# A recursive edge-list GNN kernel: a fourth pair list with its own stage, a third table of deep sums, and six matrix-power passes over 24 gather tiles in place of seven over 40

## The reference, cut to what matters

```
def step(f, _):
    msg = f[src] * edge_weight[:, None]
    agg = segment_sum(msg, dst, num_segments=n)
    return (1.0 - ALPHA) * agg + ALPHA * feat_0, None      # K = 10 steps, ALPHA = 0.1
x = layernorm(x + scan(step, x, K))
```

## Time and profile before

| what | value |
|---|---|
| median of 3 runs | 4958.19 us (4956.72 to 4958.65) |
| the profiled execution's own time | 4952.22 us |
| its span, first to last instruction | 4950.1 us |
| busy: PE, DVE, POOL, ACT | 2892, 3047, 2596, 1262 us |
| share of q1 (SP and ACT queues' DMAs), q0 (POOL's) of 16 DMA engines | 30.2%, 14.2% |

### The profile page before, as it was taken

The page is one execution under the profiler, slowest core; times in us unless marked ns, Lnnn a source line. Parts: engine busy times, 40 slices in busy tenths (PEclk is TensorE's granted clock), DMA queues, the critical chain, the costliest instruction groups (busy, mean ns, idle before and its releaser), DMA issues. The chain is left out here.

```text
span 4950.1 us, 60862 instructions
## 1 busy us (share of the span) xinstructions
PE 2892.4 (58%) x9882; PEld 1516.2 (31%) x9882; DVE 3047.2 (62%) x7896; ACT 1261.6 (25%) x3891; POOL 2596.0 (52%) x2528
## 2 busy tenths in 40 slices
PE   4700000577776999999999566656222210897665
PEld 3500000233332666666666211111111100333332
DVE  8989990788886777777777444433233326564333
ACT  0133330232332444444444111111100002342111
POOL 0067777555552233333333477747465560565776
PEclk9955555777777999999999688778555555997555
DMA  2067762899998454444444255533333324232111
GB/s 65 0 176 216 217 206 50 139 148 149 147 146 145 130 136 131 130 135 128 134 133 128 68 142 145 140 68 64 56 48 48 46 36 113 65 73 49 38 38 27
DMA packets 735672, 526.54 MB, mean 106 GB/s; under 512 B 526161, under 2 KB 647962, under 8 KB 730594
## 3 DMA queue, kind: packets, MB, share of 16 engines
q1 hardware_dynamic: 582822, 381.10, 30.2%
q0 software_dynamic: 92160, 102.50, 14.2%
q10 hardware_dynamic: 60612, 42.15, 4.0%
HBM read 270.21 MB, written 261.82 MB: 107 GB/s over the span
## 5 line engine op out<-in xcount | busy, mean ns | idle before, releaser
L1224 POOL DMA_INDIRECT out<-xob,ob x400 | 426.6, 1067 | 813.0 <-DVE xob L1327 716.5
L486 POOL DMA_INDIRECT xdst<-in_x,dstc x400 | 457.4, 1143 | 402.1 <-PEq L634 260.7
L270 POOL DMA_INDIRECT gb<-nodes,ib x400 | 393.2, 983 | 289.2 <-ACT ib L841 190.0
L259 PE MATMUL bank<-ident,act 128*99 128x128 f32 x400 | 87.1, 356 | 767.9 <-DVE act L985 698.5
L283 PE MATMUL bank<-l_chosen,l_rec 128*3 128x512 f32 x480 | 310.1, 807 | 119.3 <-DVE l_chosen L277 119.3
L290 PE MATMUL bank<-chosen,rec 128*6 128x512 bf16 x1200 | 377.9, 481 | 1.5 <-DVE chosen L277 1.5
L270 POOL DMA_INDIRECT cgb<-layer,ib x160 | 176.1, 1100 | 252.4 <-ACT ib L2102 205.2
L259 PEld LDWEIGHTS bank<-ident,act 128*99 128x99 f32 x400 | 66.4, 224 | 775.6 <-issue 775.6
L1249 PE MATMUL bank<-hm,w 128*112 128x512 f32 x600 | 301.1, 640 | 0.0
L264 PE MATMUL bank<-ident,scan 99*128 99x99 f32 (+2 forms) x1120 | 198.8, 307 | 145.6 <-DVE scan L1915 101.9
L1266 PE MATMUL bank<-bxT,w 121*128 121x512 f32 x600 | 276.5, 597 | 11.9 <-ACT bxT L1176 11.9
(11 more groups left out here) (296 smaller groups left out, 7468.3 us busy)
## 6 DMA issues: line engine op xcount, KB each, us to landing
nodes<-wt SPq DMA_DIRECT2D x40, 1286.2 KB
edges<-gb ACTq DMA_DIRECT2D x100, 194.0 KB
run_rows<-tb SPq DMA_DIRECT2D x100, 194.0 KB, 6.3
xa<-run_rows SPq DMA_DIRECT2D x100, 194.0 KB, 3.3
kb<-edge_keep SPq DMA_DIRECT2D x100, 192.0 KB
lsb<-edges SPq DMA_DIRECT2D x200, 96.0 KB
deep_sum<-bzeros SPq DMA_DIRECT2D x50, 384.0 KB
layer<-bzeros SPq DMA_DIRECT2D x50, 384.0 KB
```

What stands on the lines that cost most here:

```text
L259: last = nc.tensor.transpose(slot(dst_ps[0:w, :], t), rows_sb[:, t, c0:c0 + w], ident[:, :])
L270: yield nc.gpsimd.indirect_dma_start(out=dst[s][:, t, 0:width], out_offset=None, in_=table, in_offset=bass.IndirectOffsetOnAxis(ap=ib[s][: ...
L486: nc.gpsimd.indirect_dma_start(out=xdst[:, k * F:(k + 1) * F], out_offset=None, in_=a["x"], in_offset=bass.IndirectOffsetOnAxis(ap=dstc[:, ...
L1224: nc.gpsimd.indirect_dma_start(out=out, out_offset=bass.IndirectOffsetOnAxis(ap=ob[s][:, t:t + 1], axis=0), in_=xo[s][:, t, :], in_offset= ...
```

## The change

It adds a level. `level(2)` now takes the form that `level(1)` had (it builds list 3 and scatters its sums to `deep_sum[1]`) with two slots, `prepare(3)` follows, and `level(3)` takes the form without a list. `steps` works on list 3 and goes through six passes. The end pass scatters to a new table, `deep_sum[2]`, which is cleared beside the others and added in the merge. Tables and arrays are renamed and rotated accordingly. The core of the diff:

```
-LU = (4, 4, 2)
+LU = (4, 4, 2, 2)
-LZ = 15 * LW // P
+LZ = 19 * LW // P
...
+                      edges.rearrange("(e w) -> e w", w=PW), nodes[0:half].rearrange("(e w) -> e w", w=F)]
+        swap_rows = edges[0:half].rearrange("(e w) -> e w", w=F)
...
-        deep_sum = [dram(f"deep_sum{k}", (EP + 1, F)) for k in range(2)]
+        deep_sum = [dram(f"deep_sum{k}", (EP + 1, F)) for k in range(3)]
...
-                    for j in range(3):
+                    for j in range(LZ // ZW):
...
-                    for r in (3, 8, 12):
+                    for r in (3, 8, 12, 16):
...
                     def clear(i, s):
-                        z = (*deep_sum, *layer.values())[s]
+                        z = (*deep_sum[0:2], *layer.values())[s]
+                        if s == 0:
+                            sp.dma_start(deep_sum[2][0:EP, :].rearrange("(p r) f -> p (r f)", p=P)[:, bass.ds(i * FILL, FILL)], zeros[:, :]).then_inc(s_fill, 16)
...
-            row0, held_rows = ((0, 3), (7, 4), (11, 4))[k]
+            row0, held_rows = ((0, 3), (7, 4), (11, 4), (15, 4))[k]
-            wm = PW - 1 if k == 2 else MW
+            wm = PW - 1 if k == 3 else MW
...   (in level: every `k < 2` becomes `k < 3`, every `k == 1` becomes `k in (1, 2)`)
-                                    out=deep_sum[0], out_offset=...
+                                    out=deep_sum[k - 1], out_offset=...
...
         prepare(2, 12, 14)
-        first_rows("deep", (level_rows[2],), (idx3, oi2, w_2))
+        level(2, level_rows[1])
+        prepare(3, 16, 18)
+        first_rows("deep", (), (idx_last, own_last, w_last))
...
-        level(2, level_rows[1])
+        level(3, level_rows[2])
...   (in steps: LU[2], turns_of(eng, 2), list_keep[2] become LU[3], turns_of(eng, 3), list_keep[3])
-            one(0, level_rows[2], swap_rows, "first")
-            one(1, swap_rows, level_rows[2], "add")
-            with eng.Fori(1, (STEPS - 4) // 2) as j:
-                one(j * 2, level_rows[2], swap_rows, "add")
-                one(j * 2 + 1, swap_rows, level_rows[2], "add")
-            one(STEPS - 4, level_rows[2], None, "end")
+            one(0, level_rows[3], swap_rows, "first")
+            with eng.Fori(0, (STEPS - 6) // 2) as j:
+                one(j * 2 + 1, swap_rows, level_rows[3], "add")
+                one(j * 2 + 2, level_rows[3], swap_rows, "add")
+            one(STEPS - 5, swap_rows, None, "end")
...   (in the merge)
+                        sp.dma_start(flat(d2[s]), rows(deep_sum[2], g, 1)).then_inc(s_in[s], 16)
...
-                        dve.wait_ge(s_in[s], (i + 1) * 48)
+                        dve.wait_ge(s_in[s], (i + 1) * 64)
                         nc.vector.tensor_tensor(y[:, :, :], yb[s][:, :, :], d0[s][:, :, :], ALU.add).then_inc(s_add, 1)
-                        dve.wait_ge(s_add, g + 1)
-                        nc.vector.tensor_tensor(y[:, :, :], y[:, :, :], d1[s][:, :, :], ALU.add).then_inc(s_sum, 1)
+                        dve.wait_ge(s_add, 2 * g + 1)
+                        nc.vector.tensor_tensor(y[:, :, :], y[:, :, :], d1[s][:, :, :], ALU.add).then_inc(s_add, 1)
+                        dve.wait_ge(s_add, 2 * g + 2)
+                        nc.vector.tensor_tensor(y[:, :, :], y[:, :, :], d2[s][:, :, :], ALU.add).then_inc(s_sum, 1)
```

More of the change, by code:

```diff
@@ L175, in gnn @@
         iota_h = sb("iota_h", [P, GE], F16)
-        count = [sb(f"count{k}", [1, 1], I32) for k in range(3)]
+        count = [sb(f"count{k}", [1, 1], I32) for k in range(4)]
         def col(ap, g):
@@ L1408, in _ @@
                     drained(dve, body, 3)
-        idxb, idx3, oi2 = (sb(n, [P, NC], I32) for n in ("idxb", "idx3", "oi2"))
-        w_2 = sb("w_2", [P, NC])
+        idxb, idx_last, own_last = (sb(n, [P, NC], I32) for n in ("idxb", "idx_last", "own_last"))
+        w_last = sb("w_last", [P, NC])
         def block_of(ap, g):
@@ L1453, in level @@
                 y0 = st("y0_", F) if k == 0 else None
[L1454 to L1457, removed]
+                ds = st("ds", F, U) if k in (1, 2) else None
+                ob = slots(f"l{k}_ob", [P, T], I32, scope=scope) if k in (1, 2) else None
+                chosen = slots(f"l{k}_chosen", [P, T, GE], n=2, scope=scope) if k < 3 else None
+                packed = slots(f"l{k}_packed", [3, GE], n=2, scope=scope) if k < 3 else None
                 base = slots(f"l{k}_base", [1, 1], I32, n=U, scope=scope)
@@ L1562, in from_rows @@
                             else:
-                                nc.scalar.copy(block_of(fourth, g), psR[b][:, :, F:2 * F]).then_inc(s_cr, 1)
+                                nc.scalar.copy(block_of(settled, g), psR[b][:, :, F:2 * F]).then_inc(s_cr, 1)
                             wait(act, s_ltw[b], 16 * (i * (U // 2) + s // 2))
                             wait(act, s_lt, g - 1)
-                            if k == 1:
+                            if k in (1, 2):
                                 wait(act, s_ds, g - 1)
@@ L1725, in gnn @@
         prepare(2, 12, 14)
-        first_rows("deep", (level_rows[2],), (idx3, oi2, w_2))
+        level(2, level_rows[1])
+        prepare(3, 16, 18)
+        first_rows("deep", (), (idx_last, own_last, w_last))
         deep = ctx.enter_context(ExitStack())
-        fourth, total_2 = (deep.enter_context(nc.sbuf_tensor(n, [P, NG * T * F], F32)) for n in ("fourth", "total_2"))
-        level(2, level_rows[1])
+        settled, deep_total = (deep.enter_context(nc.sbuf_tensor(n, [P, NG * T * F], F32)) for n in ("settled", "deep_total"))
+        level(3, level_rows[2])
         def steps(runs):
-            U = LU[2]
+            U = LU[3]
             turns, turns_of, back, begun, part, drained = loops(U)
@@ L1889, in epilogue @@
                                     wait(dve, s_rst[b], (k * n + i) * (16 * (U // 2)) + s // 2 * 16)
-                                    nc.vector.tensor_tensor(rbuf[b][:, :, :], psR[b][:, :, :], block_of(fourth, g), ALU.add).then_inc(s_rb, 1)
+                                    nc.vector.tensor_tensor(rbuf[b][:, :, :], psR[b][:, :, :], block_of(settled, g), ALU.add).then_inc(s_rb, 1)
                                     nc.vector.tensor_tensor(mine, mine, psR[b][:, :, :], ALU.add).then_inc(s_acc, 1)
@@ L1958, in gnn @@
         with Scope(nc) as scope:
-            yb, d0, d1 = (slots(n, [P, T, F], scope=scope) for n in ("myb", "md0_", "md1_"))
+            yb, d0, d1, d2 = (slots(n, [P, T, F], scope=scope) for n in ("myb", "md0_", "md1_", "md2_"))
             tiles = [norm_tiles(scope, "mn", b) for b in range(2)]
```

82 lines of the change are left out of this document (41 added, 41 removed).

## The result

The changed kernel takes **4882.57 us** (median of 4 runs, 4881.47 to 4885.34), beside 4958.42 us for the kernel before on the same chip. The ratio is 0.9847, 95% interval 0.983 to 0.9864. The prediction was 4880.0 us, 2.6 us away.

The account below looks back on a forecast made before the run. POOL's count of indirect DMAs, plus fixed costs per pass and stage, sets the deep part. Terms -63.1, -100.0, -41.5, -22.1, +119.6, +13.0, +15.9 and 0 sum to -78.2 us: median 4880.0 us, range 4862 to 4908.

Parts of the forecast that it names:

- The count of POOL's indirect DMAs sets the deep part.: Deep levels and passes: time follows POOL's number of gathers and scatters, plus a fixed cost per pass and per stage.
- The new level, +119.6: New `level(2)`: ten tiles at `level(1)`'s rate plus 13.4 us before first gather and after last scatter, +119.6 us.
- ten tiles of 10.62: New `level(2)`: each of ten tiles takes 10.62 us, `level(1)`'s rate from first gather to last scatter.
- 2.4 to spare: New level: scatter landing (1.2 us) and record-to-sums (1.6) fit in the next gathers' 5.2 us, 2.4 us left.
- Rival A: New level: two-slot wait for the scatter of g-2 stalls POOL 2 to 4.5 us per tile, 4900 to 4925; chance 0.06.
- The preparation: Between levels: one more preparation, up to the next level's first load, costs +13.0 us, 12 to 15.
- The passes: Deep passes: one full pass removed, -63.1 us, and five remaining ones lose four tiles each, -100.0 us.
- 5 x 4 x 5.0: Five passes before the end pass: each loses four filled tiles of 5.0 us, -100.0 us.
- The last level, the end pass and the merge: Last level four tiles fewer, -22.1 us; end pass four fewer, -41.5; merge one dependent add more per tile, +15.9.
- Clears, 0: 100-tile pass: 25 more writes of 384 KB hide behind a full PE, 0 us, ends 0 and +10.
- rival B: 100-tile pass: DMA engines decide, the additional 9.8 MB delay PE's loads, fully exposed 74 us, about 4954; chance 0.04.
- Rivals C and D: C: list 3 needs over three turns, 4962 us, chance 0.01. D: new level runs one tile at a time, 5085, 0.04.

Follow-up runs that it names:

- c2: Changed kernel with list 3 run for two turns, four tiles a pass in place of six, on the third chip: 4773.57 us, ratio 0.9634.
- c3: Changed kernel with the new level's row numbers copied for the scatter only after the tile's row copies, third chip: 4881.73 us, ratio 0.9851.
- e3: Changed kernel with every list 3 index raised to at least its place in the tile, so rows hardly repeat; timing only, slow chip: 5258.6 us.
- e4: Changed kernel with all indices of the passes set to 0, so every gather reads row 0; timing only, slow chip: 5278.18 us.
- e7: Changed kernel plus one further level building list 4, a fourth table and five passes in place of six, slow chip: 5336.11 us, ratio 0.9963.
- c1: The changed kernel itself, run again as control on the third chip: 4882.96 us, ratio 0.9861 to the kernel before.
- e5: Changed kernel without the third table's load and add in the merge, on a slow chip: 5215.91 us.

## Why the prediction was right

*The count of POOL's indirect DMAs sets the deep part.* Right for filled tiles. POOL issued at the bare gap in the new level and through the passes, and each part moved by its count of tiles. A padding tile costs more than its issues, 7.6 us in c2, and there the landing decides.

*The new level, +119.6.* Mis-sized by 6.1 us, the largest miss: 125.7 from its first list load to the next preparation. The steady tiles ran as taken, at 10.5 us: first gather to last scatter 112.86 (3509.71 to 3622.57), less 7.43 of stalls, over ten. The edges outside them held too, 12.9 us for 13.4. The step that failed is "ten tiles of 10.62", a mean over `level(1)`, as the price of the whole loop. The "2.4 to spare" rest on the gathers of g+1 lying between two tiles' scatters, and behind the last two tiles no gathers are left. Rival A named the wait and put it at every tile; c3 shows that it costs 3.2 us, in the emptying, since elsewhere the gathers of the next tile cover it. The other stall is read from the rows as PE's order of work, the packing ahead of the transposes.

*The preparation.* +13.0 forecast and 13.4 measured (3493.24 to 3506.68).

*The passes.* -163.1 forecast, -160.1 measured. The term 5 x 4 x 5.0 was 3 us too large: a pass became 19.4 shorter (63.1 to 43.7) and not 20.0. "Tiles 8 and 9 gather one padding row over and over, and that seems to be what is slower" was right, as e3 and e4 show. It read 6.70 us a tile there and went no further: it took the padding over as given, and the padding is 15.3 us of every 43.7.

*The last level, the end pass and the merge.* Each within 2.3 us, the add at 0.39 us as the two before it.

*Clears, 0.* Right, and so rival B falls. The engines did have the work (share 0.47 before, 0.49 after in the block), and it cost no time. PE was busy 1167.5 of the block's 1220 us, so it had next to nothing to wait for. The Trainium skill ("DMA: Bandwidth & Descriptors", section "Issuing engines are not separate DMA queues") has DMAs of all issuers run on the same 16 engines; the estimated 23 us that the prediction worked out beside it would have come on top only if none of the transfer had been hidden, and all of it was.

*Rivals C and D.* List 3 took three turns, and the new level ran at 10.5 us a tile, far from 18.5.

*How close it came.* The profiles moved by 70.4 us, 7.8 less than the 78.2 of the sum. The medians moved by 75.9, because the profiled execution before lay 6.0 us below its median and the one after 1.1. So that the forecast of the median is off by only 2.6 us is in part luck; 7.8 is the size of the misses.

## What to carry to other kernels

Price a pass by the instructions of its bounding queue, padding included: a minimum number of loop turns can cost more than the optimisation around it brings (here 109 us against 76). A stage added to shorten repeated passes pays only while the passes behind it do get shorter; e7 is the same edit where they don't. Where padding can't be dropped, distinct rows for it are worth a try: e3, which spread the repeated rows of filled entries too, took 3.9 us off a pass. A mean per tile from a loop's steady part doesn't price its emptying; look there for the work that covered a wait.

## What was not expected of the hardware

A gather of one repeated row is slow. Its packets held a DMA engine 0.62 to 0.70 us each (c1's padding, e4), against 0.08 for rows that hardly repeat (e3) and 0.13 for tiles of which about half name row 0 (c1). The tile's time was then the landing, 7.0 to 7.8 us, and not POOL's issue, 5.0. Why the repeated row is slow, no run shows.

Chips differ. The same kernel before took 4955 us on one and 5313 and 5361 on two others. The PE-bound stage was as long (1151.5 us from its first scan to its last in both the kernel before and e5). `level(0)` was not: from its first scan to that of `level(1)` it took 457.2 us in c1 and 581.0 in e5. In e5 POOL waited 110.9 us of that for stores of `held` to land, in c1 not at all. What makes them land later on those chips is open. The ratio of the changed kernel to the one before was the same, within the intervals, in both measurements where the kernel before took 4955 to 4958 us. On the two slower chips it was not measured.
